# A state-space layer's chunk recurrence as scans in a turning frame, with tables and turn-backs on GpSimd

## The reference, cut to what matters

```python
x_in = x @ in_W.T + in_b;  u = swapaxes(x_in, 1, 2)
dt = exp(log_dt);  A = -exp(log_A_real) + 1j * A_imag;  dtA = A * dt[:, None]
K = exp(dtA[:, :, None] * arange(L))                 # L = 2048
Ceff = Cc * (exp(dtA) - 1) / A
k = 2 * einsum('hn,hnl->hl', Ceff, K).real           # a filter as long as the sequence
y = irfft(rfft(u, 2L) * rfft(k, 2L))[..., :L]        # causal convolution
y = gelu(y + u * D_skip[:, None], approximate=False)
```

## Time and profile before

| what | us |
|---|---|
| median of 3 runs | 340.62 (337.44, 340.62, 344.81) |
| profiled execution, its own time | 337.61 |
| its span, first to last instruction | 335.8 |
| mean granted TensorE clock | 0.918 of full speed |
| busy in the span: PE, DVE, ACT, POOL | 277.0, 224.3, 168.4, 174.9 |

### The profile page before, as it was taken

How to read it: one execution, slowest core, us unless ns; L and a number is a source line. 1 busy time by engine, 2 the same in 40 slices (tenths; PEclk the granted TensorE clock), 3 DMA queues, 4 the chain that set the end, 5 groups by cost and what they waited for, 6 DMA issues and landing times.

```text
span 335.8 us, 9262 instructions
## 1 busy us (share of the span) xinstructions
PE 277.0 (82%) x2856; PEld 247.0 (74%) x2856; DVE 224.3 (67%) x851; ACT 168.4 (50%) x340; POOL 174.9 (52%) x231
## 2 busy tenths in 40 slices
PE   1892755976698878888897999799999999999970
PEld 0891654855575556665697999699999999999920
DVE  6999998599812788888878623245556555555672
ACT  1568444589656577677746332244444444444400
POOL 2589100000190007777777775155777776777740
PEclk9998787597999989998958599999999999999995
DMA  5791028979970001111111241322423333333779
GB/s 145 209 419 41 0 72 218 265 201 288 342 203 0 0 3 49 51 56 49 57 50 56 88 131 50 95 75 66 112 74 105 96 87 110 87 98 90 274 231 278
DMA packets 54290, 41.29 MB, mean 123 GB/s; under 512 B 6215, under 2 KB 50140, under 8 KB 53744
## 3 DMA queue, kind: packets, MB, share of 16 engines
q1 hardware_dynamic: 47264, 31.20, 32.2%
q0 software_dynamic: 4544, 8.47, 7.6%
q10 hardware_dynamic: 2448, 1.20, 1.4%
HBM read 28.74 MB, written 13.02 MB: 124 GB/s over the span
## 4 chain that ended last, share of the span: by engine, by line
DVE 30%; issue 24%; PE 20%; POOL 11%; DMA 5%; ACT 3%; DVEq 3%; SPq 1%; POOLq 1%; ACTq 0%
POOL y_dram L621 8%; POOL xs_dram L615 3%; DVE u L727 2%; PE bank L1445 2%; PE bank L1661 2%; DVE stats L682 2%; PE bank L1369 2%; PE bank L1380 2%; PE bank L1672 2%; DVE st L792 2%; DMA area<-y_dram 2%; PE bank L1493 2%; DVE area L787 2%; PE bank L1393 1%; DMA cpar<-in_L_attn_C 1%
## 5 line engine op out<-in xcount | busy, mean ns | idle before, releaser
L621 POOL DMA_INDIRECT y_dram<-u x78 | 77.9, 999 | 38.2 <-issue 23.5
L615 POOL DMA_INDIRECT xs_dram<-area x64 | 62.9, 984 | 41.8 <-issue 40.3
L1000 DVE COPY v<-v 128x512 f32 x84 | 39.9, 475 | 28.9 <-issue 28.7
L1661 PE MATMUL bank<-xn,v 128*128 128x128 f32 x320 | 42.4, 275 | 0.5 <-ACT xn L1299 0.5
L1672 PE MATMUL bank<-v,xn 128*128 128x128 f32 x312 | 41.3, 275 | 0.5 <-ACT xn L1304 0.5
L1661 PEld LDWEIGHTS bank<-xn,v 128*128 128x128 f32 x320 | 38.9, 192 | 0.8 <-issue 0.7
L1672 PEld LDWEIGHTS bank<-v,xn 128*128 128x128 f32 x312 | 38.0, 192 | 0.7 <-ACT xn L1304 0.7
L1304 ACT ACTIVATE xn<-bank 128x512 f32<-128x512 f32 x40 | 23.9, 597 | 21.4 <-PE bank L1661 20.8
L1299 ACT COPY xn<-bank 128x256 f32<-128x256 f32 x41 | 15.2, 370 | 26.8 <-PE bank L1652 26.8
L1018 DVE COPY u<-area 128x2 uint32<-128x2 uint32 x39 | 6.7, 172 | 24.2 <-PE bank L1672 23.5
L1549 PEld LDWEIGHTS bank<-v 128*128 128x128 f32 x144 | 20.4, 217 | 2.3 <-issue 2.3
(11 more groups left out here) (307 smaller groups left out, 647.6 us busy)
## 6 DMA issues: line engine op xcount, KB each, us to landing
area<-kp_dram SPq DMA_DIRECT2D x12, 512.0 KB, 6.6
area<-xs_dram SPq DMA_DIRECT2D x78, 65.0 KB, 1.8
x_sb<-in_L_attn_x SPq DMA_DIRECT2D x4, 512.0 KB, 7.8
area<-ab_dram SPq DMA_DIRECT2D x2, 1024.0 KB, 5.8
xn<-ab_dram SPq DMA_DIRECT2D x2, 1024.0 KB, 10.8
xn<-kp_dram SPq DMA_DIRECT2D x4, 512.0 KB, 6.5
area<-y_dram SPq DMA_DIRECT2D x4, 512.0 KB, 5.7
area<-y_dram SPq DMA_DIRECT2D x8, 256.0 KB, 4.9
```

Source lines behind the costliest of these rows:

```text
L615: pool.indirect_dma_start(out=xs_dram.ap(), out_offset=bass.IndirectOffsetOnAxis(ap=pos[:, k, i:i + 1], axis=0), in_=hx[:, i, k, :], in_of ...
L621: pool.indirect_dma_start(out=y_dram.ap(), out_offset=bass.IndirectOffsetOnAxis(ap=ybi[:, z:z + 1].bitcast(U32), axis=0), in_=yb[:, z, :], ...
L1000: v.tensor_copy(wc[:, z % STEP], v1_flat.rearrange("p (w m) -> p w m", w=2)[:, :, bass.ds(r, HID)]).then_inc(wc_ready, 1)
L1661: last = mm(bank[2 + p % 2][:, HID * j + P * c:HID * j + P * c + P], wc[:, (2 * p + j) % STEP, 1, P * c:P * c + P], xsT[:, p % 3, P * j:P ...
```

## The change

The recurrence is done in a frame that turns with the phase of w: if S[j] = e^(i j theta) T[j], with theta the phase of w, then T[j] = |w| T[j-1] + e^(-i j theta) s[j]. The decay |w| is real, so real and imaginary parts are separate first-order recurrences, which VectorE's scan instruction does along a row. What is added and moved:

- **Tables** (GpSimd, after L579): the phase of w times j for 32 columns of modes and 16 chunks (512 elements), its cosine and sine (two sine instructions on ScalarE), the weights turned by it (`wr_t`, `wi_t`), and the decay of each mode with a zero at each row's start (`decay`). They live where the tables v1 and `area` are free, so they wait for marks such as `v1_dve` 4 and `b_ps` 1, and `table_args(3)` waits for `sine_ready` 2.
- **Per group**: `weigh_states` has four instructions (two of 512 elements from PSUM, two of 256), `scan_states` two scans of 256 elements. GpSimd turns the states of groups 0 to 2 back (two products of 512, two sums of 256, `turned_back`) and ScalarE copies them into `s_bd`; VectorE turns group 3 back by itself straight into `s_bd` (two products and eight sums on 32 partitions) and copies half of group 2.
- **Orders**: VectorE weighs and scans groups 0 to 2, norms 10 tiles, does group 3, then norms 12 more (22 in all; ScalarE keeps 10). ScalarE's `evict_k(1)` goes ahead of `sines(3)`. TensorE does `turn_tables(1)` ahead of `states(1)`; `toeplitz(0)` waits for `st_dve` 2, `toeplitz(1)` for `st_dve` 4, and `toeplitz(3)` goes behind `read_states(5)` and two transposes, so that read-outs and GELUs run group by group. SyncE's load of `hank[3]` also waits for `scanned` 4 and `turned_back` 3 (it overwrites the decay and GpSimd's buffers), and the expert weights for `sbd_dve` 1.
- The 14 steps, the three sign flips of `lw`, one argument and one cosine of a mode table go. GpSimd's additions of the output bias (L593) no longer wait for `y_ps` 1.

```diff
+            pool.wait_ge(lw_act, 1)
+            pool.wait_ge(abb_used, 2)
+            pool.wait_ge(mag_ready, 2)
+            link(tt(phase, over_chunks(3), jrow[:].unsqueeze(1).broadcast_to([P, NX, NC]), ALU.mult))
+            link(ts(turns, phase, MAGIC, None, ALU.add))
+            link(ts(turns, turns, -MAGIC, None, ALU.add))
+            tt(phase, phase, turns, ALU.subtract).then_inc(phase_ready, 1)
+            pool.wait_ge(v1_dve, 4)
+            for b in range(B):
+                ts(decay[:, :, b].rearrange(...), lw[:, 0].rearrange(...).broadcast_to([P, NG, 8, NC]), 1.0, None, ALU.mult)
...
+            link(g_.memset(area[:, 4096:5120:NC], 0.0))
+            pool.wait_ge(sine_ready, 1)
+            link(tt(half_sq, half_sq, half_sq, ALU.mult))
+            pool.wait_ge(b_ps, 1)
+            pool.wait_ge(v2_ps, 4)
+            link(ts(cos_t, half_sq, -2.0, 1.0, ALU.mult, ALU.add))
+            tt(wr_t, over_chunks(1), cos_t, ALU.mult)
+            tt(wi_t, over_chunks(5), cos_t, ALU.mult)
+            pool.wait_ge(sine_ready, 2)
+            tt(prod, over_chunks(5), sin_t, ALU.mult)
+            link(tt(half_sq, over_chunks(1), sin_t, ALU.mult))
+            tt(wr_t, wr_t, prod, ALU.add)
+            link(tt(wi_t, wi_t, half_sq, ALU.subtract))
+            g_.engine_nop().then_inc(tables_ready, 1)
+            for g in range(NG - 1):
+                s_ = group_states(g)
+                pool.wait_ge(scanned, g + 1)
+                tt(along, over_states(cos_t, g), s_, ALU.mult)
+                link(tt(across, over_states(sin_t, g), s_[:, ::-1], ALU.mult))
+                tt(s_[:, 0], along[:, 0], across[:, 0], ALU.add)
+                tt(s_[:, 1], along[:, 1], across[:, 1], ALU.subtract).then_inc(turned_back, 1)
...
+                v.tensor_tensor(s_, over_states(wr_t, g), own, ALU.mult)
+                link(v.tensor_tensor(cross, over_states(wi_t, g), own[:, ::-1], ALU.mult))
+                v.tensor_tensor(s_[:, 0], s_[:, 0], cross[:, 0], ALU.subtract)
+                v.scalar_tensor_tensor(out=s_[:, 1], in0=s_[:, 1], scalar=-1.0, in1=cross[:, 1],
+                                       op0=ALU.mult, op1=ALU.subtract).then_inc(st_dve, 1)
+            def scan_states(g):
+                dve.wait_ge(st_dve, g + 1)
+                for r in range(2):
+                    line = st[:, g, r].rearrange("p b x j -> p (b x j)")
+                    last = v.tensor_tensor_scan(line, decay[:, g].rearrange("p b m -> p (b m)"), line, 0.0, ALU.mult, ALU.add)
+                last.then_inc(scanned, 1)
+            dve.wait_ge(tables_ready, 1)
+            for g in range(NG - 1):
                 weigh_states(g)
+                scan_states(g)
+            add_norm(ACT_NORMS, ACT_NORMS + 10)
+            weigh_states(NG - 1)
+            scan_states(NG - 1)
...
-            for j in range(1, NC - 1):
-                v.tensor_tensor(m1, lr_b, sv[:, :, :, :, j - 1], ALU.mult).then_inc(dve_step, 1)
-                v.tensor_tensor(m2, li_b, sv[:, ::-1, :, :, j - 1], ALU.mult).then_inc(dve_step, 1)
...
-                link(v.tensor_tensor(sv[:, :, :, :, j], sv[:, :, :, :, j], m1, ALU.add))
-                link(v.tensor_tensor(sv[:, :, :, :, j], sv[:, :, :, :, j], m2, ALU.add))
...
+                if g < 2:
+                    pe.wait_ge(st_dve, 2 * g + 2)
...
+            for g in range(NG - 1):
+                toeplitz(g)
             for i in range(10):
+                if i == 6:
+                    toeplitz(NG - 1)
                 if i < 8:
                     read_states(i)
```

More of the change, by code:

```diff
@@ L760, in _, with add_norm @@
             table_args(3)
[L761 to L764, removed]
             products(2)
             products(3)
+            def add_norm(lo, hi):
+                for i in range(lo, hi):
+                    last = v.tensor_scalar(x_sb[:, i, :], x_sb[:, i, :], rs1p[:, i:i + 1], nmr[:, i:i + 1], ALU.mult, ALU.add)
+                return last
@@ new lines, in _ @@
+            add_norm(ACT_NORMS, ACT_NORMS + 10)
+            weigh_states(NG - 1)
+            scan_states(NG - 1)
+            along, across = halves(rnd[:, 0:512]), halves(rnd[:, 512:1024])
+            s_ = group_states(NG - 1)
+            dve.wait_ge(scanned, NG)
+            v.tensor_tensor(along, over_states(cos_t, NG - 1), s_, ALU.mult)
+            link(v.tensor_tensor(across, over_states(sin_t, NG - 1), s_[:, ::-1], ALU.mult))
+            for k in range(4):
+                for r in range(2):
+                    dst, _ = state_places(NG - 1, k, r)
+                    one, two = [t_[32 * k:32 * k + 32, r].rearrange("p b (x j) -> p b x j", j=NC)[:, :, :, 0:NC - 1]
+                                for t_ in (along, across)]
+                    last = v.tensor_tensor(dst, one, two, ALU.subtract if r else ALU.add)
@@ L1146, in _ @@
             evict_v2(0)
+            act.wait_ge(phase_ready, 1)
+            act.wait_ge(v1_dve, 4)
+            a.activation(pa.rearrange("p (x j) -> p x j", j=NC), phase, ACT.Sin, scale=PI).then_inc(sine_ready, 1)
             act.wait_ge(dskip_in, 64)
@@ L1420, in _ @@
             impulse(0)
-            for g in range(1, NG):
+            turn_tables(1)
+            states(1)
+            impulse(1)
+            for g in range(2, NG):
                 states(g)
@@ L1424, in _, with toeplitz @@
                 impulse(g)
-            pe.wait_ge(k_ready, NG)
-            pe.wait_ge(v2_act, 16)
-            pe.wait_ge(st_dve, NG)
-            for g in range(NG):
+            def toeplitz(g):
+                if g < 2:
+                    pe.wait_ge(st_dve, 2 * g + 2)
+                elif g == 2:
+                    pe.wait_ge(k_ready, NG)
+                    pe.wait_ge(v2_act, 16)
                 if g >= 2:
```

159 lines of the change are left out of this document (85 added, 74 removed).

## The result

| | us |
|---|---|
| changed kernel, median of 6 runs | 346.41 (343.87 to 348.97) |
| kernel before, 6 runs of the same comparison | 340.02 (337.44 to 344.81) |
| ratio | 1.0211, 95% interval 1.0168 to 1.0255 |
| profiled execution, its own time | 345.02, span 342.8, granted clock 0.922 |

A forecast was written before the change was run, and what follows sets the result against it. The chain to the last GELU-stage transpose (102.3), with its 19.8 us recurrence, was taken as the bound. With the port price, 92.6 + 16.2 = 108.8, 6.5 lost; between 344.1 and 347.1 the forecast was 345.5, range 341 to 350.

The forecast's parts named there:

- What bounds: Chain to the GELU stage's last transpose at 102.3, including a 19.8 us recurrence; changes there reach the end one for one.
- The port price: GpSimd and VectorE hold each other off while streaming: 1.09 us per 512-element GpSimd two-input instruction, 0.62 per one-input one.
- Part 1: GpSimd's tables beside VectorE's arguments and products: VectorE gives way 8.5 us and begins to weigh at 64.7, undisturbed 58.1.
- Part 2: VectorE's weighing, scans and ten norms to `st_dve` 4: 14.9 us plus 7.1 for GpSimd's turning back, ending at 86.7.
- Part 3: TensorE after `st_dve` 4: 5.9 us to the first read-out at 92.6, then 16.2 to the end at 108.8.
- Rival 1: Tables and turning back: GpSimd waits and VectorE doesn't, or neither does; 4 to 7 us faster, chance 0.30.
- Rival 2: TensorE's clock stays low through the read-outs, `toeplitz(1)` to last transpose: 5 to 6 us more, 12 slower, 351; chance 0.17.
- Rival 3: Scans shorten nothing because copies and `hank[3]` set the first GELUs; needs `hank[3]` 5 us later; not priced apart.

The follow-up runs named there:

- the second comparison: The changed kernel, unaltered, run again beside the kernel before on another chip than the first eight kernels: 346.89 against 338.34 us, ratio 1.0269.
- the later versions: Changed kernel with VectorE turning all states back, norms last: 398.9 us; also decay table on ScalarE: 392.5; then group 0 turned earlier, `hank[2]` needed later: 337.98, ratio 1.0005.

## Why the prediction was right, and which terms were off

It said 345.5, with 6.5 us lost at the last transpose and carried to the end; measured were 346.41, 7.0 above the kernel before, and 5.7 behind at the last transpose. The mechanism was the one that it named: GpSimd's long instructions hold VectorE off, and TensorE's second Toeplitz group waits for the last weighing. By its own steps:

- **What bounds.** That 102.3 passes to the end one for one held roughly for the loss: 5.7 there, 6.0 at the last scatter, 7.0 in the span and in the times. In the second comparison it was 6.1 there, 6.2 at the last scatter and 9.0 in the times. So 1 to 3 us more are lost behind the scatters, in a stage that the prediction took as untouched; no run shows where. It is not true of a gain: 3.35 there became 0 to 1 us until TensorE's clock was held up. The scatters run back to back only while VectorE's routing keeps ahead of them, and the prediction took this for granted in both directions.
- **The port price**, the open point, is real for products, and 0.94 for one of 512 elements rather than 1.09. For GpSimd's one-input instructions, priced at 0.62 each, it is smaller and of another kind: the two decay instructions cost VectorE three times 0.3, all of it on one-input instructions.
- **Part 1**, weighing at 64.7: measured 63.3. Its terms were off in both directions. The arguments stretched from 7.0 to 8.8 and not to about 14, since GpSimd was then in its two decay instructions, which have one input: 2.2 us each where 0.8 was taken (its bounds of 0.5 and 1.3 were both too low), and lengthened VectorE's one-input instructions by only 0.3 each. The reading products came later and met `products` instead, 4.7 to 8.05. VectorE gave way by 5.2 (1.8 + 3.4) and not 8.5, but then stood 2.5 waiting for GpSimd. So the loss was shared between the engines, which a sum for VectorE alone can't show.
- **Part 2**, 22.0 from there to `st_dve` 4: measured 21.4, of which turning back 6.9 (7.1 taken) and ten norms, scans at 0.67 and weighing as priced. It fell on scans and norms alike; the norms took 5.6 for 2.7.
- **Part 3**: 5.9 to the first read-out became 7.4, the one fall of the clock that was priced at 1.4 and left out (`toeplitz(1)` took 3.57). From there 16.0 to the end (16.2 taken). `toeplitz(3)` didn't wait for `hank[3]`.
- **Rival 1** was false as to the mechanism, and its time was wrong as well: with turning back and tables gone the mark is 99.5 and not 95.1, since TensorE stands 3.2 us for `hank[2]` and then works at the low clock (3.05 for 1.95). It starts at 80, where the prediction had seen that load landing, and it didn't carry this over to the new order. **Rival 2** was false: read-outs took 2.84 for three banks as before. **Rival 3** was false here but is what bounds the later versions: copies and a table load of 1.28 stand ahead of the first GELU.

That the total was so near has luck in it. Within part 1, 3.3 us too much for VectorE's giving way met 2.5 too little for the wait for the tables. Parts 1 and 2 together were 2.0 too much and the clock 1.5 too little. And the 0.8 by which the loss at the last transpose was forecast too high was more than made up by the 1.3 that came behind it.

## What to carry to other kernels

Work given to an idle GpSimd is not free if VectorE is on the critical path: price each long product of GpSimd at about three quarters of its own length for VectorE (0.94 of 1.27 here), and prefer writes beside two-input VectorE work. When a step is taken off the critical path, work out the next two things that will be waited for (here a load and another engine's copies) before naming the gain. And a stage that passes a delay on in full may swallow a gain, so follow it to the end of the program.

## What the runs showed of the hardware

- Where GpSimd's eight products ran beside VectorE's arguments, both engines lost: VectorE 0.94 for each of the seven instructions that it met (13.5 for 7.0 in all), GpSimd 0.54 (1.81 for 1.27).
- A memset of 1152 elements (1.44 us) stretches VectorE's one-input instructions of 1024 by 0.6 to 0.9, and leaves the two-input one at 1.29.
- GpSimd's one-input multiplication of a broadcast array of 512 elements takes 2.2 us beside VectorE's work, longer than a two-input product (1.28 in the first row of GpSimd above, beside VectorE too). What it takes alone wasn't measured.
- TensorE's granted clock went to 0.50 behind a wait of only 1.25 us within a busy stage, and stayed at 1.00 behind one of 1.28 earlier in the same trace. Products put in such waits held it at 1.00 at both places where it had fallen; with them it fell at 148 to 150 instead.
- One chip gave 399 us for the kernel before in two comparisons and 340 in the last; why its later stages were longer is open.
